# Second attention of a two-layer graph network: Vector engine splits values by upper halves, Scalar engine packs them, eight far source tiles instead of six

## The reference

```python
seq = (x @ W_seq).reshape(N, H, DH)                   # N 2048, H 16 heads, DH 32
scores = score1[:, :, None] + score2[:, None, :]      # per head: s1[i] + s2[j]
scores = leaky_relu(scores, negative_slope=0.2) + (1.0 - adj)[None] * MASK_VAL
attn = softmax(scores, axis=-1)
hidden = einsum('hij,jhd->ihd', attn, seq).reshape(N, 512)
```

## Time and profile before

| | us |
|---|---|
| median of 3 runs (1329.02 to 1330.25) | 1329.88 |
| the profiled execution's own time | 1327.29 |
| its span, first to last instruction | 1325.7 |
| VectorE busy in the span | 974.9 |
| ScalarE busy in the span | 797.1 |
| TensorE granted clock, mean over the span | 0.942 of full |

### The profile page before, as it was taken

How to read it: one execution, slowest core, us unless ns; L and a number is a source line. 1 busy time by engine, 2 the same in 40 slices (tenths; PEclk the granted TensorE clock), 3 DMA queues, 4 the chain that set the end, 5 groups by cost and what they waited for, 6 DMA issues and landing times. The chain is left out here.

```text
span 1325.7 us, 24575 instructions
## 1 busy us (share of the span) xinstructions
PE 1152.6 (87%) x10450; PEld 784.7 (59%) x10450; DVE 974.9 (74%) x1340; ACT 797.1 (60%) x779; POOL 169.9 (13%) x182
## 2 busy tenths in 40 slices
PE   4797668889888888888699399999999999999797
PEld 3343323333333333334355299999999999999543
DVE  2310137999999999988189679999889988999265
ACT  1321526556665556553144588888888888888032
POOL 2777700000000000000066100000000000000011
PEclk9899789998898898899899699999999999999799
DMA  9530151221112110000476210000110000000321
GB/s 358 73 25 1 20 113 18 42 42 37 39 34 42 34 35 34 17 16 24 128 177 109 74 34 34 34 34 34 44 55 34 34 34 34 34 34 3 112 111 71
DMA packets 31625, 75.00 MB, mean 57 GB/s; under 512 B 5413, under 2 KB 10402, under 8 KB 29474
## 3 DMA queue, kind: packets, MB, share of 16 engines
q1 hardware_dynamic: 21426, 49.53, 10.7%
q0 software_dynamic: 10096, 23.97, 10.5%
HBM read 78.76 MB, written 15.61 MB: 71 GB/s over the span
## 5 line engine op out<-in xcount | busy, mean ns | idle before, releaser
L959 ACT ACTIVATE s_masks<-s_s1b,s 128x2048 fp8e4<-128x2048 f32 x208 | 396.7, 1987 | 0.0
L1104 PE MATMUL psum<-s_V,s_masks 128*128 128x198 bf16 x2560 | 352.3, 249 | 15.2 <-DVE s_masks L1001 15.2
L1105 PE MATMUL psum<-s_V,nadjT 128*128 128x99 bf16 x2560 | 347.0, 209 | 0.0
L1104 PEld LDWEIGHTS psum<-s_V,s_masks 128*128 128x128 fp8e4 x2560 | 249.9, 98 | 15.7 <-issue 15.4
L1105 PEld LDWEIGHTS psum<-s_V,nadjT 128*128 128x128 fp8e4 x2560 | 250.2, 98 | 0.0
L461 PE MATMUL psum<-h,s_WT 128*128 128x512 f32 x512 | 246.1, 606 | 0.6
L502 ACT ACTIVATE s_exp<-s_exp,s_negm 128x1536 f32<-128x1536 f32 x96 | 150.7, 1570 | 101.3 <-DVE s_negm L597 101.3
L441 PE MATMUL psum<-f_qk 64*128 64x512 f32 x576 | 159.5, 693 | 54.9 <-DVE s_negm L597 54.9
L1001 DVE TENSOR_TENSOR s_masks<-s_masks,adjT 128x512 uint32<-128x512 uint32 x256 | 169.4, 681 | 49.5 <-ACT s_masks L959 47.0
L597 DVE CUSTOM_DVE_ANT_0 s_exp<-psum,f_low 128x1536 f32<-128x1536 f32 x96 | 164.7, 1752 | 16.7 <-PE psum L441 16.2
L588 DVE SCALAR_TENSOR_TENSOR s_W<-s_exp,s_r,s_W 128x1536 f32<-128x1536 f32 x96 | 174.4, 1817 | 2.2
(11 more groups left out here) (127 smaller groups left out, 1140.5 us busy)
## 6 DMA issues: line engine op xcount, KB each, us to landing
s_s1b<-s_rows SPq DMA_DIRECT2D x16, 1024.0 KB, 4.6
s_adj<-in_adj POOLq DMA_DIRECT2D x16, 512.0 KB, 5.2
rel_planes<-s_zero POOLq DMA_DIRECT2D x3, 2304.0 KB, 23.0
f_rel<-rel_planes SPq DMA_DIRECT2D x36, 192.0 KB, 3.5
s_x<-x SPq DMA_DIRECT2D x6, 1024.0 KB, 11.0
h<-in_x SPq DMA_DIRECT2D x4, 1024.0 KB, 21.1
f_adj<-in_adj POOLq DMA_DIRECT2D x16, 256.0 KB, 5.5
s_x<-in_x SPq DMA_DIRECT2D x16, 256.0 KB, 2.6
```

The costliest lines, as they stand in the source:

```text
L959: act.activation(masks[:, j, :], s1b[b][:, :], ACT.Relu, bias=t["s2"][:, n, 0, j:j + 1], scale=BIG, saturate=False).then_inc(signs, 1)
L1104: pe.matmul(out, masks[:, j, cols], V[:, b, j, :, :], **first)
L1105: last = pe.matmul(out[:, :, DZ:CZ], nadjT[:, j, cols], V[:, b, j, :, DZ:CZ], **then)
```

## The change

`tmp` becomes two buffers, and `upper` is a view of the upper 16 bits of every f32 in them, read as bf16 with a step of two elements. The high part is now this upper half (cut off, not rounded). VectorE subtracts it itself, into the second buffer, and then subtracts that buffer's upper half to give the low part. ScalarE's two instructions per head (now `pack`) copy the upper halves into `V` at any later time; TensorE waits for both. `pack` is at j = 9 and 14 in place of 5 and 11. `FAR` has 8 tiles, tile 0 among them. On VectorE the small pieces move to other j, and `invert` and `norm` now stand next to each other.

```diff
-FAR = (1, 4, 6, 9, 11, 14)
+FAR = (0, 3, 5, 7, 9, 11, 13, 14)
...
-    tmp = sb("tmp", [P, NT, CZ])
+    tmp = sb("tmp", [P, 2, NT, CZ])
+    upper = tmp[:, :, :, :].bitcast(BF16).rearrange("p s j (c w) -> p s j c w", w=2)[:, :, :, :, 1]
...
-            def part(m, b, p):
+            def pack(m, b, p):
 
                 act.wait_ge(*((value, 2 * (m + 1)) if p == 0 else (rest, m + 1)))
                 if p == 0 and m >= 2:
                     act.wait_ge(psum_done[1], m - 1)
-                act.activation(V[:, b, :, p, :], tmp[:, :, :], ACT.Copy).then_inc(hi_out if p == 0 else mid_out, 1)
+                act.activation(V[:, b, :, p, :], upper[:, p, :, :], ACT.Copy).then_inc(packed, 1)
...
-                    if j in (5, 11) and n < HB - 1:
-                        part(n + 1, 1 - b, 0 if j == 5 else 1)
+                    if j in (9, 14) and n < HB - 1:
+                        pack(n + 1, 1 - b, 0 if j == 9 else 1)
...
             def values(m):
 
                 if m > 0:
-                    dve.wait_ge(split, m)
+                    dve.wait_ge(packed, 2 * m - 1)
+                    dve.wait_ge(rest, m)
...
-                dve.wait_ge(hi_out if p == 0 else mid_out, m + 1)
-                out = tmp[:, :, :] if p == 0 else V[:, b, :, 2, :]
-                dve.tensor_tensor(out, tmp[:, :, :], V[:, b, :, p, :], ALU.subtract).then_inc(rest if p == 0 else split, 1)
+                dve.wait_ge(*((value, 2 * (m + 1)) if p == 0 else (rest, m + 1)))
+                if p == 0 and m > 0:
+                    dve.wait_ge(packed, 2 * m)
+                    dve.wait_ge(split, m)
+                if p == 1 and m >= 2:
+                    dve.wait_ge(psum_done[1], m - 1)
+                out = tmp[:, 1, :, :] if p == 0 else V[:, b, :, 2, :]
+                dve.tensor_tensor(out, tmp[:, p, :, :], upper[:, p, :, :], ALU.subtract).then_inc(rest if p == 0 else split, 1)
...
-                        if j == 2:
+                        if j == 3:
                             sum_parts(n - 1, 0)
                         if j == 5:
                             sum_parts(n - 1, 1)
-                        if j == 7:
+                        if j == 13:
                             scale(n - 1)
-                        if j == 8:
+                        if j == 14:
                             join(n - 1)
-                        if j == 9:
+                        if j == 15:
                             invert(n - 1)
-                        if j == 11:
                             norm(n - 1)
                     if n < HB - 1:
                         if j == 1:
                             values(n + 1)
-                        if j == 6:
+                        if j == 9:
                             take_off(n + 1, 1 - b, 0)
-                        if j == 12:
+                        if j == 11:
                             take_off(n + 1, 1 - b, 1)
...
                 pe.wait_ge(split, n + 1)
+                pe.wait_ge(packed, 2 * (n + 1))
```

More of the change, by code:

```diff
@@ L925, in stage4 @@
         sem("signs"), sem("vector_signs"), sem("mask"), sem("far"), sem("mask_used"))
-    value, hi_out, rest, mid_out, split = sem("value"), sem("hi"), sem("rest"), sem("mid"), sem("split")
+    value, rest, split, packed = sem("value"), sem("rest"), sem("split"), sem("packed")
     psum_done, bank_free = ([sem(f"{n}{i}") for i in range(2)] for n in ("psum_done", "bank_free"))
@@ L960, in head @@
                                        saturate=False).then_inc(signs, 1)
-                    if j in (5, 11) and n < HB - 1:
-                        part(n + 1, 1 - b, 0 if j == 5 else 1)
-            part(0, 0, 0)
-            part(0, 0, 1)
+                    if j in (9, 14) and n < HB - 1:
+                        pack(n + 1, 1 - b, 0 if j == 9 else 1)
+            pack(0, 0, 0)
+            pack(0, 0, 1)
             for n in range(HB):
@@ L975, in values @@
                 if m > 0:
-                    dve.wait_ge(split, m)
-                dve.tensor_tensor(tmp[:, :, :].rearrange("p j (k z) -> p j k z", k=2)[:, :, :, 0:DH],
-                                  seq[:, :, None, m * DH:(m + 1) * DH].to_broadcast([P, NT, 2, DH]),
+                    dve.wait_ge(packed, 2 * m - 1)
+                    dve.wait_ge(rest, m)
+                out = tmp[:, 0, :, :].rearrange("p j (k z) -> p j k z", k=2)
+                dve.tensor_tensor(out[:, :, :, 0:DH], seq[:, :, None, m * DH:(m + 1) * DH].to_broadcast([P, NT, 2, DH]),
                                   t["e"][:, :, :, m:m + 1].rearrange("p k j o -> p j k o").to_broadcast([P, NT, 2, DH]),
                                   ALU.mult).then_inc(value, 1)
-                dve.tensor_copy(tmp[:, :, :].rearrange("p j (k z) -> p j k z", k=2)[:, :, :, DH:DZ],
-                                t["e"][:, :, :, m:m + 1].rearrange("p k j o -> p j k o")).then_inc(value, 1)
+                dve.tensor_copy(out[:, :, :, DH:DZ], t["e"][:, :, :, m:m + 1].rearrange("p k j o -> p j k o")).then_inc(value, 1)
             def take_off(m, b, p):
-                dve.wait_ge(hi_out if p == 0 else mid_out, m + 1)
-                out = tmp[:, :, :] if p == 0 else V[:, b, :, 2, :]
-                dve.tensor_tensor(out, tmp[:, :, :], V[:, b, :, p, :], ALU.subtract).then_inc(rest if p == 0 else split, 1)
+                dve.wait_ge(*((value, 2 * (m + 1)) if p == 0 else (rest, m + 1)))
[6 more added lines that the diff above has]
+                dve.tensor_tensor(out, tmp[:, p, :, :], upper[:, p, :, :], ALU.subtract).then_inc(rest if p == 0 else split, 1)
             def vector_sign(n, b, j):
```

## The result

The changed kernel takes 1305.99 us (median of 4 runs, 1304.86 to 1306.76) against 1330.07 for the one before, run beside it. The ratio is 0.9818, with a 95% interval of 0.9801 to 0.9835. It is faster by 24.1 us where 20.8 were forecast, and the time lies near the low end of the forecast's range of 1304 to 1317.

What follows compares the result with a forecast made beforehand. TensorE was taken to bound heads 1 to 15; 18.3 us from two more far tiles plus 2.5 from the first head, 20.8 in all, takes the median from 1329.88 to 1309 us; range 1304 to 1317.

Steps and rivals of the forecast that it cites:

- the thinnest cover: VectorE's work per head, with two added XORs, put at 28.2 to 28.5 us, 0.3 to 0.6 below TensorE's 28.78.
- TensorE's head: Heads on TensorE: two more far tiles save 1.22 us each head, 30.00 to 28.78; 18.3 us over 15 heads.
- a fifth of a microsecond: TensorE's waits in a middle head: none for anyone beyond this size, so TensorE was taken as the bound.
- The first head: Head 0: TensorE starts 2.1 us later, a 3.4 us mask wait goes; gain 2.5 us, bounds 1 to 4.5.
- the lower clock: Head 0 on TensorE: extra time from the reduced granted clock, taken as 3.1 us, bounds 1.9 to 3.5.
- The split: Stepped upper halves: VectorE's subtraction stays 1.17 us start to start, ScalarE's copy 0.99; at most twice that.
- rival (b): VectorE's subtractions: stepped upper halves halve their rate, heads 30.6 us, 1337 us in all; chance 0.05.
- (a): VectorE becomes the bound in the heads: 29.3 us a head gives 1317 us, 29.0 gives 1312; chance 0.12.
- (c): TensorE's weight loads set its pace: heads stay near 30.0 us, time 1327 to 1330; chance 0.03.
- (d): Signs still hold VectorE, the two XORs only fill its idle time, TensorE starves for masks; about 0 gain; chance 0.02.

## Why the prediction was right, and by how much

The step that carried it held: TensorE bounds the heads, and two far tiles take columns off it at a fixed price per pair. The far tiles that it called hidden on VectorE were hidden, by 0.3 us, the low end of the 0.3 to 0.6 that it named as the thinnest cover.

**The term that was too small** is TensorE's head: 28.78 forecast, 28.51 measured. Of the 0.27 us, 0.21 is the wait for tile 6's XOR, shown by exchanging that tile; the prediction had seen it as "a fifth of a microsecond" and taken it for nothing, and its sentence that it doesn't matter which tiles are far was wrong for this tile. It was the end of a chain through three engines that starts when TensorE ends a head: ScalarE's copy, sign 6, mask 6, subtraction, sign 8, mask 7, XOR 6, 7.4 us in all, against 7.4 us of TensorE's steps. Two parts of the change bear on it. Tile 6 is no longer far, which was enough by itself in the old order. And in the new order ScalarE has made the signs to 9 by then. No run has the new order with tile 6 far and without GpSimd's work beside it, so the share of each stays open; an estimate from the trace after is that the new order would be enough too: mask 7 ends at 997.09, an XOR of tile 6 behind it would end about 997.7, and TensorE's step of tile 6 starts at 998.97. The other 0.06 is the price of a pair, 38 ns read from 24 pairs against 40 ns by whole heads. The wait stood in 14 heads and the price counts in 15, so together this is 3.9 us.

**The first head** was forecast to gain 2.5 us. TensorE's first matmul came at 760.19 - 3.54 = 756.65 on the clock of the kernel before, forecast 756.5; the signs at 751.29, forecast 751.3. Head 0 ended at about 791.6, which is 2.8 us less into the stage than before. That this is so near to 2.5 is partly luck. The forecast had 28.8 us of steps and 3.1 us for the lower clock, 31.9, and the head took 31.4; but the 3.1 is not what was there. At a granted clock of 0.50 TensorE did only tile 0 and tile 1: 760.19 to 761.51 and on to 763.39, 1.32 and 1.88 us where such steps take 0.735 and 1.04 at 1.00. So the clock cost about 1.4 us, under the forecast's lower bound of 1.9. The XORs of tiles 3, 5 and 11, which the forecast counted as in time, cost about as much: by the starts of matmuls around them 0.6, 0.2 and 0.5 us. A term taken too large and one left out cancelled.

Against the gain of the first head stand 0.62 us lost at the seam to head 1, which the prediction did not have: it took VectorE's arrival at the sums from a steady head, while VectorE leaves the first one late. Sum: from the end of head 0 to the end of head 15 TensorE took some 449.8 us before and 428.5 after, 21.3 less, and 2.8 more from head 0: 24.1.

**The split** was costed at no change for either engine, and both prices held (1.25 and 1.07 us). The forecast did not claim a gain for it; the runs show none, alone (0.9995) or with the new order (470.00 against 469.90 us). The stepped operand, rival (b), has no place: L994 was 1.25 us in all rows. The Trainium skill (SBUF — State Buffer, Door 1: The DMA port swizzle) had such a read free while at least two accesses fall into one 16-byte line, and the trace agrees.

**The other rivals.** (a), VectorE as the bound, is true of the first heads' sums, where VectorE comes late, without costing TensorE more than that 0.62 us, and becomes true in full with a ninth tile. (c), weight loads: TensorE's weight loads are busy in all 28.51 us, as in 29.82 of 30.00 before, with as many loads; a measure that stays full while the head gets 5% shorter does not say what bounds it. The Trainium skill (Perfetto Trace Analysis, Identifying the Most-Contended Engine), which the prediction set beside this rival, names MFU, the arithmetic done as a share of the peak, next to the share of weight loads; the prediction gave only the second half. (d), that far tiles only fill VectorE's idle time, is nearest to what the old order does, where VectorE's stands for signs remain and the gain is 10 us of 24.

## What to carry to other kernels

A wait of 0.2 us with no name, in 14 heads of 16, is a term: look what ended on the other engines just before it, and exchange that one item to prove it. When a piece of work is moved between engines or split anew, test the order and the trick apart; here the order and the far tiles carried everything that could be measured. When a sum comes out right, check its terms one by one: in the first head two wrong ones cancelled. Where two engines meet within 1%, the next gain is in balancing all of them at once.

## What was not expected of the hardware

Two-operand work on GpSimd and VectorE did not run side by side here: beside GpSimd's 1.97 us `scale`, VectorE's mask took 2.45 us in place of 0.68, so it stood for nearly all of it. It ended 0.55 us behind `scale`, and the XOR 0.54 us behind `join`. The Trainium skill (SBUF — State Buffer, Who interferes with whom) says that the second input of a VectorE instruction with two inputs in SBUF comes through a read interface shared with GpSimd, and that the shared pair is an exclusive lock; the trace agrees. Whether VectorE's instructions with one input in SBUF, or its sums from PSUM, are spared can't be read here: none of them ran beside GpSimd's work. Moving 2.4 us of such work off VectorE gave it 3.5 us of standing (1.77 + 0.92 at these two rows, and 0.85 at the XOR beside `norm`, 1.53).

It was also not plain from the forecast that the first head would be indifferent to TensorE's start: 1.6 us earlier gave nothing.
